# The last three feed-forward jobs of a graph-attention kernel: bias by TensorE, inner rows in the score bank, two pairs of banks, edge rows normalised on VectorE

## The reference, cut to what matters

```
q, k, v = h @ Wq, h @ Wk, h @ Wv
e   = sum over a head of k[src] * q[dst] / sqrt(64);  attn = softmax of e over edges of one dst
o   = segment_sum(attn * v[src], dst) @ Wo
y   = layernorm(h + o) * ln1_g + ln1_b
f   = relu(y @ W1 + b1) @ W2 + b2                 # W1 is 512x64, W2 is 64x512
out = layernorm(x + layernorm(y + f) * ln2_g + ln2_b)   # the last one without gain and bias
```

## Time and profile before

| | |
|---|---|
| median of 3 runs | 696.63 us (696.45 to 697.27) |
| the profiled execution | 701.9 us, its span 700.2 us |
| busy in the span | PE 638.2 (91%), DVE 577.0 (82%), ACT 533.9 (76%), POOL 398.1 (57%) |
| mean granted TensorE clock | 0.957 of full speed |
| last work of the chain | the scatters into `out_dram` by POOL, after `z9` on DVE |

### The profile page before, as it was taken

The page is one execution under the profiler, slowest core; times in us unless marked ns, Lnnn a source line. Parts: engine busy times, 40 slices in busy tenths (PEclk is TensorE's granted clock), DMA queues, the critical chain, the costliest instruction groups (busy, mean ns, idle before and its releaser), DMA issues. The chain is left out here.

```text
span 700.2 us, 10740 instructions
## 1 busy us (share of the span) xinstructions
PE 638.2 (91%) x3450; PEld 487.6 (70%) x3450; DVE 577.0 (82%) x1389; ACT 533.9 (76%) x1151; POOL 398.1 (57%) x363
## 2 busy tenths in 40 slices
PE   3899999999999899999999999999999999967740
PEld 2788877787777677777777777776777777645520
DVE  7658679968898698898889889888898897997672
ACT  1525269978898787988898898879779987997781
POOL 7084354674576655756776575572746374566223
PEclk9999999999999999999999999999999999996755
DMA  7743164555435825663482466446555543655432
GB/s 232 205 114 114 31 149 91 161 118 143 139 97 171 184 67 146 167 147 89 155 187 89 135 176 149 90 157 119 143 127 159 111 105 132 120 119 147 85 66 88
DMA packets 37746, 91.42 MB, mean 131 GB/s; under 512 B 8346, under 2 KB 9642, under 8 KB 37690
## 3 DMA queue, kind: packets, MB, share of 16 engines
q0 software_dynamic: 31536, 82.74, 46.3%
q1 hardware_dynamic: 6154, 8.01, 4.1%
HBM read 71.20 MB, written 20.99 MB: 132 GB/s over the span
## 5 line engine op out<-in xcount | busy, mean ns | idle before, releaser
L530 ACT ACTIVATE squares<-rows,nmean 125x512 bf16<-125x512 f32 x200 | 142.2, 713 | 41.0 <-DVE nmean L857 20.2
L391 POOL DMA_INDIRECT out_dram<-rows,node_idx x40 | 45.9, 1148 | 56.6 <-ACT rows L585 47.1
L445 POOL DMA_DIRECT2D x_rows<-in_L_gnn_ln_b_dram x40 | 53.3, 1375 | 42.2 <-DVE rows L788 28.9
L387 POOL DMA_INDIRECT x_rows<-in_x_dram,node_idx x40 | 45.6, 1140 | 55.6 <-DVE rows L872 41.0
L853 DVE SCALAR_TENSOR_TENSOR rows<-pF,rows 125x512 f32<-125x512 f32 x80 | 51.9, 685 | 24.9 <-PE pF L1027 19.7
L918 PE MATMUL pP<-wo_hi,aT_hi 128*125 128x512 f32 x160 | 66.3, 415 | 0.1
L918 PE MATMUL pP<-xTs_hi,wv_hi 128*128 128x500 f32 x160 | 66.3, 414 | 0.0
L918 PE MATMUL pP<-xTd_hi,wq_hi 128*128 128x500 f32 x160 | 65.6, 410 | 0.0
L918 PE MATMUL pP<-wo_lo,aT_hi 128*125 128x512 f32 x160 | 63.5, 397 | 0.0
L918 PE MATMUL pP<-xTs_hi,wk_hi 128*128 128x500 f32 x160 | 63.5, 397 | 0.0
L918 PE MATMUL pP<-wo_hi,aT_lo 128*125 128x512 f32 x160 | 63.4, 396 | 0.0
(11 more groups left out here) (179 smaller groups left out, 1774.8 us busy)
## 6 DMA issues: line engine op xcount, KB each, us to landing
x_rows<-in_L_gnn_ln_b_dram POOLq DMA_DIRECT2D x40, 512.0 KB
dst_row<-in_dst_dram SPq DMA_DIRECT2D x9, 250.5 KB
q<-in_L_gnn_Wq_dram SPq DMA_DIRECT2D x1, 1024.0 KB, 5.7
rows<-in_L_gnn_Wk_dram SPq DMA_DIRECT2D x1, 1024.0 KB
rows<-in_L_gnn_Wv_dram SPq DMA_DIRECT2D x1, 1024.0 KB, 8.5
x_rows<-in_L_gnn_Wo_dram SPq DMA_DIRECT2D x8, 128.0 KB
xd<-in_x_dram,dst_idx POOLq DMA_INDIRECT x40
xs<-in_x_dram,src_idx POOLq DMA_INDIRECT x40
```

What stands on the lines that cost most here:

```text
L387: pool.indirect_dma_start(rows, None, x, bass.IndirectOffsetOnAxis(ap=table[:, column:column + 1].bitcast(U32), axis=0), bounds_check=N - ...
L391: pool.indirect_dma_start(out, bass.IndirectOffsetOnAxis(ap=table[:, column:column + 1].bitcast(U32), axis=0), rows, None, bounds_check=N ...
L445: pool.dma_start(xr_wide[n], bass.AP(tensor=be2.tensor, offset=be2.offset, ap=[[0, P], [0, 2], [1, D]]), accum_op=ALU.add).then_inc(s[f"be ...
L530: ins = act.activation(squares[:, t, :], w[n][:, t, :], ACT.Square, bias=nmean[c][n][:, t:t + 1], accum_out=sq[c][n][:, t:t + 1])
```

## The change

In the last three jobs of round 9 (E0, E1, N0; the code has them as `closing`):

- The bias comes by PE: step `B9` multiplies the identity with `bias_all` into both output banks, `start=True`. ACT's `seed` and the seed behind the relu are left out.
- The inner rows go into `pS` (the bank of the scores, whose last use is over), each job to columns of its own (`hidden`).
- The output banks are `pF`, then `pP[0:2]`, then `pF` again (`f_banks`); `B9` of the second job waits for all H steps (`hx_done`), that of the third for `x2` of the first.
- E0 and E1 are normalised on DVE (`norm9`), not on ACT; E0's last norm goes back from DVE (`z9`) to ACT (`z`).

The due times are new from round 0 on, so steps change places elsewhere too. PE's list is the same up to round 8's TXD0, ACT's to about the same place. DVE's has two swaps of neighbours in rounds 2 to 4. POOL's has SAVE behind BIAS and round 1's GXD. In rounds 8 and 9 many steps move.

```diff
-SLOT_PERIOD = {"N0": 7684, "N1": 7682}
+SLOT_PERIOD = {"N0": 7683, "N1": 7685}
...
-!SAVE -69250; !BIAS -46200; GXD -201076 -32352 122318 122634 124465; GXS -86453 38598 129311 131967 131899;
+!SAVE 15608; !BIAS -46200; GXD -201076 -32352 122318 122662 124531; GXS -86453 38598 129311 130950 129750;
...
+        closing = [(i, step.split(".")[0]) for i, step in pe_steps if step.endswith(".F19")]
+        def hidden(i, slot):
+            n = closing.index((i, slot))
+            return pS[:, R * n:R * n + R]
+
+        def f_banks(i, slot):
+            return pP[0:2] if (i, slot) == closing[1] else pF[::-1]
...
+                    elif what == "F19":        # ACT
+                        before = job_before(i, slot)
+                        on.wait_ge("f_filled", 2 * nth("pe.F2", before[1], before[0]))
+                        on.wait_ge("h_filled", nth("pe.F1", slot, i))
+                        act.activation(hT[:, :], hidden(i, slot), ACT.Relu, bias=b1_col[:, :]).then_inc(s["h_done"], 1)
...
+                    elif what == "norm9":      # DVE
+                        on.wait_ge("nb1_done", nth("dve.r1", slot, i))
+                        on.wait_ge(f"out_{slot}", 32 * i)
+                        rows = xr[n] if slot[0] == "N" else w[n]
+                        for t in range(2):
+                            ins = dve.tensor_scalar(w[n][:, t, :], rows[:, t, :], rs[1][n][:, t:t + 1], nb1[n][:, t:t + 1],
+                                                    ALU.mult, ALU.add)
+                        ins.then_inc(s["last_n1_done"], 1)
...
+                    elif what == "B9":         # PE
+                        before = closing.index((i, slot))
+                        on.wait_ge("bias_loaded", 16)
+                        on.wait_ge("ident_done", 1)
+                        if before == 1:
+                            on.wait_ge("hx_done", 4 * ROUNDS)
+                        else:
+                            j, old = job_before(i, slot) if before == 0 else closing[0]
+                            on.wait_ge("x2_done", 2 * nth("dve.x2", old, j))
+                        for bank in f_banks(i, slot):
+                            pe.matmul(bank[0:R, :], ident[0:R, 0:R], bias_all[0:R, :], start=True, stop=True)
+                    elif what == "F19":        # PE
+                        on.wait_ge("nT_done", 2 * nth("act.T", slot, i))
+                        on.wait_ge("weight_exp", ROUNDS)
+                        if closing.index((i, slot)):
+                            j, old = job_before(i, slot)
+                            on.wait_ge("h_done", nth("act.F1", old, j))
+                        for k in range(KC):
+                            for t in range(2):
+                                ins = pe.matmul(hidden(i, slot)[DFF * t:DFF * t + DFF, :], w1[:, k, :], nT[:, k, R * t:R * t + R],
+                                                start=(k == 0), stop=(k == KC - 1))
+                        ins.then_inc(s["h_filled"], 1)
+                    elif what == "F29":        # PE
+                        on.wait_ge("h_done", nth("act.F1", slot, i))
+                        for t in range(2):
+                            pe.matmul(f_banks(i, slot)[t][0:R, :], hT[DFF * t:DFF * t + DFF, :], w2[DFF * t:DFF * t + DFF, :],
+                                      start=False, stop=True, skip_group_check=True).then_inc(s["f_filled"], 1)
```

More of the change, by code:

```diff
@@ L31 @@
[L31 to L35, removed]
@@ L46 @@
[L46 to L50, removed]
@@ L51 @@
[L51 to L66, removed]
+!HQ -299672; !HK -100416; !HV -82111; !HO -39217; TXD0 -126220 -10760 125712 125374 125114;
+TXS0 -98802 24316 131158 131052 131445; Q0 -86658 43928 131621 131047 130453; V0 34194 127287 136963 137053 168307;
@@ L80 @@
[L80 to L84, removed]
@@ new lines @@
+FI 15610 113768 132148 137563 164529; GN0 71434 141576 142836 141895 218130; GE0 101354 138305 140544 141278 207969;
+GN1 33235 136637 139663 140229 168595; GE1 137046 139955 142071 147597 228361; mask 29948 84661 131262 135008 158870;
+N0.be 146112 148981 147856 187736 255091; N0.out 149610 152159 152660 240814 379749;
+N1.be 136724 139979 144858 155109 209286; N1.out 145571 148297 148812 188508 256564;
+E0.be 141767 140438 145165 171034 241864; E0.out 146710 149038 150473 190412 267420;
+E1.be 142340 144267 145283 181195 255109; E1.out 147856 150997 151501 239387 305343
@@ L276, in graph_attention @@
         pe_steps = sequence("pe")
-        turns = [(i, step, half) for i, step in pe_steps if step[:2] == "TX" or step.endswith(".T")
-                 for half in range(2 if step.endswith(".T") else 1)]
+        turns = [(i, step, half) for i, step in pe_steps if step[:2] == "TX" or step.endswith((".T", ".T9"))
+                 for half in range(1 if step[:2] == "TX" else 2)]
         turn = {key: n for n, key in enumerate(turns)}
@@ L281, in graph_attention @@
         place = {key: n for n, key in enumerate(products)}
-        jobs = [(i, step.split(".")[0]) for i, step in pe_steps if step.endswith(".F1")]
+        jobs = [(i, step.split(".")[0]) for i, step in pe_steps if step.endswith((".F1", ".F19"))]
         job = {key: n for n, key in enumerate(jobs)}
+        closing = [(i, step.split(".")[0]) for i, step in pe_steps if step.endswith(".F19")]
+        assert len(closing) == 3 and closing == jobs[-3:]
+        assert all(products[-1] in pe_steps[:pe_steps.index((i, f"{slot}.B9"))] for i, slot in closing[1:])
+        def hidden(i, slot):
[3 more added lines that the diff above has]
+            return pP[0:2] if (i, slot) == closing[1] else pF[::-1]
         def pT_of(i, step, half=0):
@@ L1003, in _ @@
                     n = SLOTS.index(slot)
-                    if what == "T":
-                        on.wait_ge("n1_done", nth("act.norm", slot, i))
+                    if what in ("T", "T9"):
+                        if ("act.norm", slot, i) in steps_done:
+                            on.wait_ge("n1_done", nth("act.norm", slot, i))
+                        else:
+                            on.wait_ge("last_n1_done", nth("dve.norm", slot, i))
                         for half in range(2):
```

169 lines of the change are left out of this document (104 added, 65 removed).

## The result

The changed kernel takes 689.05 us (median of 4 runs, 687.82 to 689.9); in the same session the kernel before took 696.54 (4 runs, 695.21 to 697.27). The ratio is 0.9898 (95% interval 0.9878 to 0.9918), 7.5 us faster by the medians. The forecast was 688.8.

The account below looks back on a forecast made before the run. PE bounds mid-kernel, a chain the last 60 us. 2.3 us of lead left at E0's x2, 8.2 at the last x2, 8.1 at z9, less 0.3 at POOL: 696.63 − 7.8 = 688.8 us; range 685.0 to 695.5.

Parts of the forecast that it names:

- O earlier: Products O0 to O3 of round 9 on PE: O0 starts 8.0 us earlier, O3 ends 5.8 us earlier.
- The work put off: Round 8's t, y, squares and norms, now between O0 and the last jobs, leave 2.3 of 5.8 us at E0's x2.
- The last jobs: E0, E1, N0 in round 9: ACT has about 5.4 us less work; the last x2 ends 8.2 us earlier.
- Half clock in the tail: PE at half clock in the tail: each B9 taken at 2.1 us, about 0.6 of N0's showing.
- Rival 3: In the tail PE keeps its full clock: gain 10.8 us, 685.8 us; chance 0.10.
- The end: Last x2 to z9 takes 8.9 us (8.8 before); the 11.8 us behind stay but for 0.3; gain 7.8.
- SAVE: POOL's fill_nodes write in the head, issued from 41.61, lands at 44.1: cost 0, bounds 0 and 5.0 us.
- Rival 1: In the head the fill_nodes write lands late; PE stands 5.0 us at 62, its clock halves: 695.8 us; chance 0.11.
- The stop in mid-kernel: PE's 2.67 us wait up to 232.86, then half clock: part of the profiled execution's 5.3 us over the median.
- Rival 4: In the tail N0's norm may wait 0.5 to 2 us for round 8's scatter: gain 7; no separate chance.
- Rival 2: In the tail ACT stays the bound, O's lead is lost wholly: gain 3 to 4 us, 693; chance 0.17.
- Rounds 1 to 8: Ahead of the tail, DVE swaps only neighbours, PE keeps its list and sets the pace: cost 0.

Follow-up runs that it names:

- E0: Not a follow-up run: a job of the kernel, the first of the last three jobs of round 9; no time of its own as a kernel.
- e2: Changed kernel's job code and lists from E0's round 9 transposes on, everything ahead in the order of the kernel before: 688.43 us, ratio 0.9903.
- e9: Changed kernel's order, but the last three jobs in the old form (ACT seeds and bias copies, one pair of banks, no bias product): 692.49 us.
- e6: Changed kernel with the norms of E0 and E1 back on ACT instead of DVE: 692.18 us, ratio 0.9946.
- e11: Changed kernel with E0's last norm on DVE again, ahead of N0's t, not on ACT: 690.37 us, ratio 0.9912.
- e5: Changed kernel without the three bias products, each F2 opening its banks itself: 687.86 us, ratio 0.9893.
- e3: Changed kernel with one pair of output banks for all three last jobs, E1's bias product right ahead of its F2: 689.22 us, ratio 0.9914.
- e4: Changed kernel with SAVE where it was before, ahead of BIAS and round 1's gathers: 688.25 us, ratio 0.9895.
- e1: Kernel before with V3 and O products earlier on PE, t, r2, y of round 8's N0 and E1's t behind L3 on DVE: 701.77 us.
- e10: e1 plus N1's relu ahead of round 8's E1.z on ACT, and N1's x2 and m2 behind H0, H1 and E0's m1 on DVE: 703.45 us.
- e12: e2 plus N0's relu ahead of E1's squares, E1's third squares ahead of E0's z, N0's m3 ahead of E1's r3: 690.45 us.
- e8: Changed kernel with N0's relu ahead of E1's squares, E1's third squares ahead of E0's z, N0's m3 ahead of E1's r3: 690.40 us.

## Why the prediction was right, point by point

**O earlier: right in size.** L3 of round 9 ends at 627.1 (before 637.4 − 5.0, so 5.3 earlier, as summed from 4.1 and 1.2), O0 starts 7.8 earlier (8.0 said), O3 ends at 642.8, 5.0 earlier (5.8 said).

**The work put off: the step that failed.** I wrote "most of the 5.8 is lost again: 2.3 remain at this point". x2 of E0 ends at 655.3 where it was 656.1: 0.8 remain, and e2 has the same x2 without any lead, so nothing of the lead remains. The reason I gave, squares and norms of round 8 on ACT, is half of it. The chain shows the other half: N1's F2 stands behind O2, and N1's x2 waits 2.7 us for it on DVE. Behind that x2 stands N0's `m3` (round 8), for which ACT waits until 641.78; from there on ACT is busy without a break, and E1's squares end at 649.3. Only then can DVE do E1's `r1` and norm, then `t` of N1, and behind these E0's x2, 2.9 us after its F2 was done. I had let F1 and F2 of N1 cost PE 2.2 us and never asked who waits for the F2 that was moved, nor what stands ahead of E0's x2 on DVE.

**The last jobs: right mechanism, mixed sizes.** The three x2 end 6.6 and 5.0 us apart (7.1 and 5.5 said, 8.5 and 10.0 before). In the sum I had 8.2 us at the last x2, 2.3 of lead and 5.9 of shorter distances; measured are 7.7, 0.8 and 6.9. The parts, by the tail distance and by ratios: old job form 2.7 and 3.8 (e9), norms on DVE 3.6 and 3.3 (e6), E0's z on ACT 1.0 and 1.0 (e11), bias product nothing and 0.4 (e5), second pair 0.2 and 1.1 (e3). Without the last two, that is 7.3 and 8.1, around the 7.0 to 7.5 of the whole. I never priced the two norms by themselves. So most of the lead that I counted and did not get was made good by the parts of the jobs: a sum that comes out right with a term that is wrong, and to that extent luck.

**Half clock in the tail: wrong, and without effect.** I took B9 at 2.1 us at half clock and 0.6 of N0's on the path. It took 1.88 (E0's) and 1.98 us (N0's) at full clock and 2.93 for E1's, part of it at half (652.82, clock 0.65), so 2.1 was no upper bound; N0's lay wholly in the wait for the relu. The clock was 0.91 from 640 to 660 and 1.00 from 656 to 665. I had written that it was 0.50 in all of the tail before; my own rows say 0.84 from 640 to 660. Rival 3 promised 3 us more for a full clock, which didn't come, since after x2 of E0 the chain runs on DVE, ACT and POOL.

**The end: right in the main.** From the last x2 to the last z9 it took 9.5 us (8.9 said), yet the end is set by E1's z9 and four scatters, which I had as "E1's two scatters and N0's in one run": 7.0 of gain at the end by the traces, 7.8 said.

**SAVE: right.** These are POOL's rows of the changed kernel:

```profile
39.49 0.60 POOL L443 DMA_DIRECT2D fill_nodes<-att  x1
42.97 1.02 POOL L448 DMA_INDIRECT edge_idx<-fill_nodes,fill_idx  x1 [2.89 <-DMA fill_nodes<-att]
```

The write landed 2.7 us after its issue, FI began at 42.97, ahead of the 45.0 that I had set as the bound, and PE's transposes of `xs` started at 62.64 without a wait. Rival 1 is out, and e4 shows that the place has no price.

**The stop in mid-kernel** was an incident of one execution and not of the kernel (5.0 us between the traces, 5.3 said; e1 and e10, which have the lists of the kernel before up to there, come to the transposes at 291.2 and 291.4), so taking the gain off the median was right. **Rival 4**: N0's norm (ACT, 653.54) had no wait for the scatter issued until 650.97. **Rival 2** was right that the lead is lost wholly and the second pair buys little, and wrong in its price of 3 to 4 us: it left out the norms. **Rounds 1 to 8** cost nothing: from 100 to 600 PE is busy for 499.5 of 500 us.

## What to carry to other kernels

Where an early product is bought by moving a step behind it, follow that step's own readers: here a matmul of 1.1 us moved behind others cost its reader on another in-order engine 2.7 us, and the whole lead of 5 us was gone at the next job. Ask of each result what stands ahead of its reader in the reader's own list: E0's x2 came 2.9 us after its F2. To take a few steps of a new order without the rest is no test of that order: e1 and e10 did so and lost 6 to 7 us, with no lead in the products at all. And look for the end at the engine that ends the kernel: behind a queue of equal scatters it is not the last result that counts, but the first one from which the queue runs without a break.

## What the runs showed of the hardware

The small write of `fill_nodes` (19.5 KB) took 8.4 to 9.3 us from issue to landing in five profiles where POOL issued it at about 26.5 us, among the weight loads (before, e1, e2, e10, e12), 2.7 to 3.0 us in eight where it stands at 39.4 to 41.5 (the changed kernel, e3, e5 to e9, e11), and 1.8 us in e4, where it was issued at 24.53. So the same write differs by a factor of 5 with its moment. The load at that moment differs too: in the kernel before, the share of the DMA engines was 0.73 from 27 to 28 us and 0.99 from 28 to 29, right behind the issue; in e4 it was 0.08 and 0.09 in the two us from 24 on and rose to 0.74 only at 27, when the write had landed; in the changed kernel it fell from 0.77 (40 to 41) to 0.28 and then 0 under the write. That the load makes the wait fits all three and was not tested by itself. The Trainium skill's fixed cost of about 2 us for a DMA (page "DMA: Bandwidth & Descriptors", section "Latency and other measured facts") fits the quiet cases (1.8 to 3.0) and misses the busy one (8.4 to 9.3).

With the three bias products left out (e5) the granted clock was 0.50 from 650 to 656, with them 0.72, and the transposes and F1 there took 1.93 us where the changed kernel's later ones took 1.07 and 1.08: the time saved by leaving out work off the chain was taken back in part by the clock. e3, which has no bias product at that place either, ran E1's transposes and F1 in 1.81 and 1.94 us, and e4 and e8, which have it, at full clock (1.07 and 1.08, the product between them 1.88). That it was the products that kept the clock up is likely and not shown: the changed kernel has the lists of e4 and its product took 2.93.
